# A graph network's set-up: edge words moved by xor and minimum, weights by predicated copies, x's norms in between

## The reference, cut to what matters

```
x: (6250, 256)   src, dst: (106250,) int32, sorted by dst   edge_weight: (106250,)
h   = layernorm(x)                       # rows: mean, variance, eps 1e-5
msg = logmap(h[src], h[dst]) * edge_weight[:, None]
agg = segment_sum(msg, dst)
u   = expmap(agg, h) ...                 # then a Mobius product with weight, bias
# three more layers: attention with a softmax per node, scores, a mean
```

## Time and profile before

| | us |
|---|---|
| three runs, median (lowest, highest) | 4950.73 (4947.53, 4952.23) |
| span of the profiled execution | 5717.0 |
| busy in it: PE, DVE, ACT, POOL | 3330.2, 3248.6, 1811.1, 3290.0 |
| mean granted TensorE clock | 0.754 of full |
| first gather, first sum added to A | 155.88, 240.59 |

### The profile page before, as it was taken

How to read it: one execution, slowest core, us unless ns; L and a number is a source line. 1 busy time by engine, 2 the same in 40 slices (tenths; PEclk the granted TensorE clock), 3 DMA queues, 4 the chain that set the end, 5 groups by cost and what they waited for, 6 DMA issues and landing times. The chain is left out here.

```text
span 5717.0 us, 56211 instructions
## 1 busy us (share of the span) xinstructions
PE 3330.2 (58%) x11120; PEld 2187.6 (38%) x11120; DVE 3248.6 (57%) x10255; ACT 1811.1 (32%) x4253; POOL 3290.0 (58%) x3410
## 2 busy tenths in 40 slices
PE   0477777777543555556554555555555556666555
PEld 0355555555431333333333333333333334333333
DVE  8677777777983555555566344444447344334435
ACT  2254444444692323333336322222226100000000
POOL 5566666666004666666653666666662466666664
PEclk8789988898875777776777767777777776667767
DMA  2444444443114333333333444444443433333333
GB/s 90 118 110 111 110 110 107 110 111 106 49 46 123 92 91 93 94 89 93 92 101 119 111 111 113 114 112 112 114 111 114 143 98 99 93 98 101 99 91 107
DMA packets 290665, 586.90 MB, mean 103 GB/s; under 512 B 63201, under 2 KB 170717, under 8 KB 290334
## 3 DMA queue, kind: packets, MB, share of 16 engines
q0 software_dynamic: 159456, 440.74, 29.6%
q1 hardware_dynamic: 100322, 108.64, 6.1%
q10 hardware_dynamic: 30556, 33.94, 2.1%
HBM read 530.98 MB, written 52.10 MB: 102 GB/s over the span
## 5 line engine op out<-in xcount | busy, mean ns | idle before, releaser
L519 POOL DMA_INDIRECT X<-table,src_tab x2490 | 2367.7, 951 | 1786.5 <-issue 690.4
L639 PE MATMUL psum<-X,onehot 128*128 128x259 f32 x4980 | 1906.8, 522 | 1245.7 <-DVE A L1280 570.9
L639 PEld LDWEIGHTS psum<-X,onehot 128*128 128x128 f32 x4980 | 1118.2, 251 | 1827.8 <-issue 1117.1
L1280 DVE SCALAR_TENSOR_TENSOR A<-A,psum 128x259 f32 x1660 | 701.7, 423 | 1315.4 <-remote 690.8
L1280 DVE SCALAR_TENSOR_TENSOR A<-A,same_tab,psum 128x259 f32 x1620 | 777.0, 480 | 613.4 <-remote 308.3
L509 POOL DMA_INDIRECT X<-table,src_tab x832 | 793.7, 954 | 534.0 <-issue 233.1
L780 ACT ACTIVATE onehot<-G,zero_col,ecols 128x128 f32<-128x128 bf16 x1660 | 697.3, 482 | 987.6 <-remote 325.5
L648 PE MATMUL psum<-H,G 128*128 x1664 | 602.9, 450 | 352.9 <-DVE G L1368 208.9
L626 PE MATMUL psum<-X,onehot 128*128 128x259 f32 x1664 | 559.3, 422 | 4.4 <-DVE A L1280 3.1
L648 PEld LDWEIGHTS psum<-H,G 128*128 128x128 f32 x1664 | 318.1, 215 | 545.5 <-issue 510.0
L780 ACT ACTIVATE onehot<-onehot,zero_col,coef 128x128 f32<-128x128 bf16 x832 | 350.6, 482 | 277.3 <-DVE coef L1411 83.7
(11 more groups left out here) (367 smaller groups left out, 2843.4 us busy)
## 6 DMA issues: line engine op xcount, KB each, us to landing
X<-table,src_tab POOLq DMA_INDIRECT x3322
plain<-rows_dram ACTq DMA_DIRECT2D x168, 160.0 KB
plain<-rows_dram SPq DMA_DIRECT2D x104, 256.0 KB
table<-H SPq DMA_DIRECT2D x21, 906.5 KB, 5.9
x_dram<-X SPq DMA_DIRECT2D x21, 896.0 KB, 4.1
X<-x_dram SPq DMA_DIRECT2D x14, 896.0 KB, 6.1
table<-A SPq DMA_DIRECT2D x7, 906.5 KB, 7.0
G<-x_dram SPq DMA_DIRECT2D x7, 896.0 KB
```

The costliest lines, as they stand in the source:

```text
L519: pool.indirect_dma_start(ring[:, s % SLOTS, :], None, table, bass.IndirectOffsetOnAxis(src_tab[:, s:s + 1], 0)).then_inc(sem(f"batch_in{s ...
L639: pe.matmul(psum[:, k % ACC_BANKS, 0:W], hots[:, k % HOTS, :], ring[:, k, :], start=True, stop=True).then_inc(sem("used"), 1)
L1280: stt(total, total, same, psum[:, t % ACC_BANKS, 0:W], ALU.mult, ALU.add).then_inc(sem("sum_added"), 1)
```

## The change

The words become positive f32 bit patterns: a mark at bit 29, an "empty" bit at 27 and the distance's seven bits in reverse order from bit 20 to 26, above the 13 bits of src. A level is an xor with its bit into `movers[i]` and a minimum of that with what stands at the place 2^i to the left. The level's mover is kept; ScalarE turns the seven into masks with a Relu (of -1 times the word plus a constant), and VectorE moves the weights by seven predicated copies, in place of GpSimd. The new fields() reverses the bits with integer operations on VectorE. Statistics, roots, norms and squares of x stand between the levels, in order 0 to 6; ScalarE squares five parts, VectorE two. dst goes out first on SP's queue, src on ScalarE's between x's parts 0 and 1; parts 2 to 6 wait for dst. The raw weights load early into onehot, are transposed before the words, and are copied by ScalarE, as are rows_out. GpSimd zeroes 3787 of A's 12691 columns. cuts_made and links_made, weight_columns and node_scalars run within g = -3, -2 and -1 of layer 0's loop, on VectorE; SP stores the cuts ahead of the fifth load of rows; VectorE waits for them before g = 0. The loop's own steps are as before.

```diff
+X2_ACT = 5 * UN
...
+MARK = 1 << 29
+EMPTY = 1 << 27
+TOP = 26
+ARRIVED = struct.unpack("f", struct.pack("I", MARK | 1 << TOP - 6))[0]
...
+            rows_in(sp, dst, dst_rows_i[:, :, 0:P], "dst_padded", 1, "dst_in")
...
+            sp.dma_start(wide["bb"], bias0.rearrange("(p d) -> p d", p=1).to_broadcast([P, D])).then_inc(sem("bias_in"), 16)
+            for n, w in enumerate((w0, w1, w_neigh, w_self)):
+                sp.dma_start(wraw[:, n], w.rearrange("(c p) d -> p c d", p=P)).then_inc(sem("raw_in"), 16)
+            rows_in(sp, edge_weight, w_rows[:, :, P:2 * P], "sums_zero", 1, "w_in")
...
+            for c in range(OUTER):
...
+                if f == 4:
+                    steps_out()
...
-            pool.memset(A[:, :, :], 0.0).then_inc(sem("sums_zero"), 1)
...
-                for i, low in enumerate(LOW):
-                    shift = 1 << i
-                    pool.wait_ge(sem("movers"), i + 1)
-                    pool.wait_ge(sem("w_kept"), 2 * i + 1)
-                    now, to = w_rows[:, :, low:], w_rows[:, :, low - shift:2 * P - shift]
-                    pool.tensor_copy(moved_w[i], movers[i]).then_inc(sem("w_taken"), 1)
-                    pool.wait_ge(sem("w_taken"), 2 * i + 1)
-                    pool.tensor_tensor(moved_w[i], now, moved_w[i], ALU.mult).then_inc(sem("w_taken"), 1)
-                    pool.wait_ge(sem("w_taken"), 2 * i + 2)
-                    pool.tensor_tensor(now, now, moved_w[i], ALU.subtract).then_inc(sem("w_kept"), 1)
-                    pool.wait_ge(sem("w_kept"), 2 * i + 2)
-                    pool.tensor_tensor(to, to, moved_w[i], ALU.add).then_inc(sem("w_kept"), 1)
...
+            pool.memset(a_flat[:, EW:2 * EW], 0.0).then_inc(sem("sums_zero"), 1)
+            pool.memset(a_flat[:, left:NB * W], 0.0).then_inc(sem("sums_zero"), 1)
...
+            x_part(0)
+            rows_in(act, src, src_rows_i, "src_padded", 1, "src_in")
+            x_part(1)
...
+            act.wait_ge(sem("dst_in"), 16 * (3 + EC))
+            for c in range(2, OUTER):
+                x_part(c)
...
+            for c in range(OUTER):
+                act.wait_ge(sem("rstd_ready"), c + 1)
                 for b in part(c):
                     norm_first(b)
+                if c + 1 < OUTER:
+                    root_first(c + 1)
...
+                if c == 2:
+                    act.wait_ge(sem("weights_turned"), 1)
+                    for n, name in enumerate(("w0T", "w1T", "wnT", "wsT")):
+                        ins = act.copy(wT[name][:, :, 0:D], psum[:, 4 + n, :].rearrange("p (c d) -> p c d", c=2))
+                    ins.then_inc(sem("weights_kept"), 1)
+
+            act.wait_ge(sem("words_moved"), 1)
+            for i in range(len(LOW)):
+                func(movers_f[i], movers_f[i], ACT.Relu, bias=col("t3")[:, i:i + 1], scale=-1.0).then_inc(sem("masks"), 1)
+            act.wait_ge(sem("dst_turned"), 1)
+            act.copy(rows_out[:, 0:4, :], psum[:, 0, :].rearrange("p (c e) -> p c e", c=4))
+            act.copy(rows_out[:, 4:6, :], psum[:, 1, 0:2 * P].rearrange("p (c e) -> p c e", c=2))
+            act.copy(rows_out[0:S - 6 * P, 6, :], psum[0:S - 6 * P, 1, 2 * P:3 * P]).then_inc(sem("rows_kept"), 1)
...
-            for i, low in enumerate(LOW):
-                shift = 1 << i
-                now, to = words[:, :, low:], words[:, :, low - shift:2 * P - shift]
-                taken = moved[:, 0:EC * (2 * P - low)].rearrange("p (c e) -> p c e", c=EC)
-                chain(ts(movers[i], now, SRC_BITS + i, 1, ALU.logical_shift_right, ALU.bitwise_and))
-                chain(tt(taken, now, movers[i], ALU.mult))
-                dve.sem_inc(sem("movers"), 1)
-                if i + 1 < len(LOW):
-                    chain(tt(now, now, taken, ALU.subtract))
-                    chain(tt(to, to, taken, ALU.add))
...
+            def fields():
+
+                SHL, SHR, AND, OR = ALU.logical_shift_left, ALU.logical_shift_right, ALU.bitwise_and, ALU.bitwise_or
+                dve.wait_ge(sem("dst_in"), 16 * (3 + EC))
+                chain(ts(delta_i, dst_rows_i[:, :, 0:P], P - 1, MARK >> SRC_BITS, AND, OR))
+                dve.tensor_copy(last_dst, dst_rows_i[:, :, P - 1])
+                tt(gone_i, dst_rows_i[:, :, 0:P], dst_rows_i[:, :, 1:P + 1], ALU.not_equal)
+                chain(ts(half_a, delta_i, 4, 0x70, SHL, AND))
+                chain(stt(half_a, delta_i, 4, half_a, SHR, OR))
+                chain(stt(half_a, delta_i, 8, half_a, AND, OR))
+                ts(half_b, half_a, 2, 0x44, SHL, AND)
+                chain(stt(delta_i, gone_i, EMPTY.bit_length() - 1 - SRC_BITS, delta_i, SHL, OR))
+                chain(stt(half_b, half_a, 0x2A, half_b, AND, OR))
+                chain(ts(half_a, half_a, 2, 0x11, SHR, AND))
+                chain(tt(half_b, half_b, half_a, OR))
+                chain(stt(delta_i, half_b, TOP - 6 - SRC_BITS, delta_i, SHL, OR))
+                dve.wait_ge(sem("src_in"), 16 * 3)
+                chain(stt(words[:, :, P:2 * P], delta_i, SRC_BITS, src_rows_i, SHL, OR))
+
+            def move(i):
+
+                low, shift = LOW[i], 1 << i
+                chain(ts(movers[i], words[:, :, low:], 1 << TOP - i, None, ALU.bitwise_xor))
+                to = words_f[:, :, low - shift:2 * P - shift]
+                chain(tt(to, to, movers_f[i], ALU.min))
...
             first_stats(0)
-            for n in range(1, OUTER):
-                first_stats(n)
-                first_rstd(n - 1)
-            first_rstd(OUTER - 1)
-
-            def add_left(out_, at, shift):
-
-                for a, z in tabs:
-                    b = a + shift
-                    ins = tt(out_[:, a:z], out_[:, a:z], psum[:, at + b // 512, b % 512:b % 512 + z - a], ALU.add)
-                return ins
+            first_rstd(0)
+            fields()
+            first_stats(1)
+            move(0)
+            first_rstd(1)
+            move(1)
+            first_stats(2)
+            move(2)
+            first_rstd(2)
+            move(3)
+            first_stats(3)
+            move(4)
+            first_rstd(3)
+            move(5)
+            first_stats(4)
+            move(6)
+            dve.sem_inc(sem("words_moved"), 1)
+            first_rstd(4)
+            first_stats(5)
+            first_rstd(5)
+            first_stats(6)
+            first_rstd(6)
...
+                from_next = psum[:, 2 + (a + 1) // 512, (a + 1) % 512:(a + 1) % 512 + z - a]
+                ts(arrived[:, a:z], from_next, ARRIVED, None, ALU.is_lt)
+                ins = tt(words_tab_f[:, a:z], words_tab_f[:, a:z], from_next, ALU.min)
...
+            chain(ts(field_tab, words_tab, SRC_BITS, MARK >> SRC_BITS, ALU.logical_shift_right, ALU.bitwise_xor))
+            chain(ts(dst_tab[:, :], field_tab, float(P), None, ALU.min))
+            dve.sem_inc(sem("tables_kept"), 1)
...
+            dve.wait_ge(sem("w_in"), 16 * 3)
+            for i, low in enumerate(LOW):
+                shift = 1 << i
+                dve.wait_ge(sem("masks"), i + 1)
+                if i:
+                    dve.wait_ge(sem("w_moved"), i)
+                dve.copy_predicated(w_rows[:, :, low - shift:2 * P - shift], movers[i], w_rows[:, :, low:]).then_inc(sem("w_moved"), 1)
+
+            dve.wait_ge(sem("x2_dve"), NB - X2_ACT)
+            dve.wait_ge(sem("x2_act"), X2_ACT)
+            dve.tensor_copy(col("x2"), H[:, :, AUX2])
+            dve.sem_inc(sem("rows0_free"), 1)
...
+            for a, z in tabs:
+                ins = dve.copy_predicated(w_tab[:, a:z], arrived[:, a:z],
+                                          psum[:, 4 + (a + 1) // 512, (a + 1) % 512:(a + 1) % 512 + z - a])
+            chain(ins)
+            dve.wait_ge(sem("table_stored"), 16 * OUTER)
+            dve.tensor_copy(H[:, :, AUX], col("x2")).then_inc(sem("own_squares"), 1)
...
+            def cuts_made():
+                dve.wait_ge(sem("rows_kept"), 1)
+                chain(dve.memset(cuts_out, 0.0))
+                tt(cuts_out[:, 0:EC - 1, 1:P], rows_out[:, 0:EC - 1, 1:P], rows_out[:, 0:EC - 1, 0:P - 1], ALU.not_equal)
+                n = S - (EC - 1) * P
+                chain(tt(cuts_out[0:n, EC - 1, 1:P], rows_out[0:n, EC - 1, 1:P], rows_out[0:n, EC - 1, 0:P - 1], ALU.not_equal))
+                ts(cuts_out, cuts_out, -BIG, None, ALU.mult)
...
+            bias_scaled()
             for g in range(-3, NG0):
+                if g == 0:
+                    dve.wait_ge(sem("steps_out"), 16 * (EC + 1))
                 if g >= 0:
...
+                    if g == -3 and k == 12:
+                        cuts_made()
+                        links_made()
+                    if g == -2 and k == 12:
+                        weight_columns()
+                    if g == -1 and k == 0:
+                        node_scalars()
```

More of the change, by code:

```diff
@@ L9 @@
+import struct
 from contextlib import ExitStack
@@ L237, in gnn_program @@
-        o += EC * P // 2
```

(45 more changed lines are left out.)

270 lines of the change are left out of this document (114 added, 156 removed).

## The result

The changed kernel takes 4917.36 us (four runs, 4916.38 to 4919.76) against 4950.69 (four runs): a ratio of 0.9935, 95% interval 0.9922 to 0.9947. It is 33 us faster, where 71 were forecast, and lies outside the range of 4852 to 4902. This time the profiled execution's span, 4914.3 us, is as long as the runs.

The account below looks back on a forecast made before the run. Layer 0's loop start was taken as the bound: set-up terms summed to a first addition at 150.3 against 219.5 without stalls, 69.2 us, taken as 71. So 4950.7 - 71 = 4880 us, range 4852 to 4902.

Parts of the forecast that it names:

- The bound: Layer 0's loop: its start, the first addition at 240.59, decides; GpSimd's 24.89 us wait at the full ring confirms it.
- Rival 3: Layer 0's gathers pace it, so only their stream's 59.6 us earlier start is won: 4891 us, chance 0.12.
- A term put at nothing: Layer 0's loop and all behind it: taken as untouched, so no change of time was counted there.
- The words: VectorE's set-up: 66.4 + 4.4 us removed, 17.6 for levels and 12.1 for fields() added, 41 us less.
- When fields() starts: VectorE's set-up: fields() at 24.5 us, about as now (24.09), with bounds 20 and 29; ScalarE free at 22.4.
- Squares, masks, copies: Set-up before layer 0: ScalarE's seventh square ends at 80.7; masks cost nothing; seven predicated copies 8.6 us, upper bound 17.
- The stalls: Before layer 0's loop: without stalls of 6.4 and 14.7 us the start is 219.5; change worth 69.2, or 90.3 if real.

Follow-up runs that it names:

- the second profile: The kernel before, unchanged, run and profiled again beside the kernel after on one chip: 4953.35 us, with a span of 4951.5.
- tt_on_pool: The kernel after with one cast and one multiplication of 32 columns added on GpSimd behind its memsets: 4895.11 us, 0.9889 of the kernel before.
- no_pool_moves: The kernel before without GpSimd's weight moves, so layer 0's weights are other numbers: 4940.8 us, 0.9978 of the kernel before.
- x_by_sp: The kernel after with x's parts 2 to 6 and the tail issued by SP behind dst instead of by ScalarE: 4903.46 us, 0.99.

## Why the prediction was wrong

Two steps failed, and both stand in one sentence: "Layer 0's loop, and all behind it, is untouched, so the change is worth what it moves the loop's start".

**The bound: wrong.** I took the 24.89 us wait at the full ring for the sign that the loop's start decides, and it belonged to a profiled execution 766 us longer than the runs. Undisturbed, that wait is 2.38 us, gathers follow each other with 0.30 between them through the whole layer, and the stream's start decides. Rival 3 described it, with 59.6 us and a chance of 0.12; measured are 55.5 and the 2 of the ring's wait. I had asked of each stall whether a run without profiler has it, and removed the stalls from the set-up, but not from the loop's pace, where they hid the bound. The first profile's view of the gathers has them:

```profile
L509 POOL DMA_INDIRECT X<-table,src_tab x832: 940/946/1838, 155.9 to 1431.5; - x167
...
  PE psum L626: 157.5, 72
  remote: 92.3, 43
```

That is 1.54 us from gather to gather, where it is 1.26 in the second profile.

**A term put at nothing: the step that cost most.** The loop's instructions are the same, but not their durations. I costed the removal of GpSimd's weight moves as a gain in contention only; it also changed what GpSimd had run before the gathers, and that made each gather dearer. Of the start's gain, 12.7 us are lost within layer 0 (10.6 in the table, and the ring's wait that is gone) and 11.9 within layers 1 to 3. The sum is then 55.5 + 2.1 - 12.7 + 1.0 - 11.9 = 34.0, of 33.9.

**What each was worth.** From the 71 to the 34, 1.8 is what I had put on top of 69.2 for the stalls; 5.8 is the loop's start, 63.4 earlier and not 69.2; 5.8 is the bound, 57.6 for the stream and the ring in place of 63.4; 23.6 is the dearer gathers, less the 1.0 won between layers 0 and 1. With the bound wrong and the gathers at their old price the time would have been 4950.7 - 57.6 = 4893, within the range. tt_on_pool is that kernel: its gathers have the old medians, and it is 57.9 us faster than the kernel before on its chip (4953.0 - 4895.1).

**The words: right.** Levels at 1.08 to 1.55 an operation, fields() 11.9 from 31.63 to 43.53 (12.1 in the sum), and no_pool_moves shows the contention by itself: 30.6 of the 66.4 us.

**When fields() starts: mis-sized.** 31.6, not 24.5, and past the bound of 29. ScalarE was free at 29.6, not at 22.4: dst, for which it waits behind the first part of x, was in at 13.67, not at 10.5, and five parts and the tail then took 15.9 us, not 11.9. Of the 7.2 us, 3.2 are dst's and 4.0 the issues'. Through ScalarE's other work 7 us became 5: last rstd at 86.1 (forecast 81.1), src_tab done at 90.4 (85.1), first gather 101.4 (96.3). x_by_sp shows what waiting for these issues costs in all, 14 us.

**Squares, masks, copies: right.** ScalarE ends the chain of x (3.60 us idle before the last rstd, as laid out). The masks take 7.32 from 90.0, beside VectorE's work, and VectorE has only 0.22 idle before the copies; what the masks would have cost on VectorE, no run tried. The seven copies take 9.87 against 8.6, at 17 the range's end was far. The first addition is at 155.7 to 156.5 against 150.3: 5 of it from fields().

**The stalls: right.** 219.5 was the estimate of the undisturbed start, 219.89 is what the new profile shows. They were the profile's, neither kernel has them.

## What to carry to other kernels

A profile that is much longer than the runs is to be taken again before any bound is read from it: its stalls fall on all engines, but they hide best the one that works at a fixed pace. Look then for an engine whose gaps are all equal; where there is one, count from its first instruction and not from where its results are used. And work that is taken off an engine may change what its other instructions cost, as it did here, where that was two thirds of the miss: compare the medians of unchanged instructions first.

## What the runs showed of the hardware that was not expected

A gather issued by GpSimd takes 957 ns in the median (951 at the least) when only iotas, a select and memsets ran before it, and 946 (942) once a cast or a two-input operation has run, also with a memset behind the cast. The 49 scalings that GpSimd does between layers 1 and 2 raise 946 to 953 and leave 957 as it is; a cast and a product behind them bring it back to 946. By the medians tt_on_pool should win 1662 gathers at 11 ns and 1660 at 4, an estimate of 25 us, and it won 22 to 26. Why is open: the runs show what sets the duration, not what it is inside GpSimd, and the cast alone or the product alone behind the scalings was not tried.

ScalarE issued the first two parts of x (at 0.81 and 4.14 us) in 0.43 and 0.41 us. Of the five parts from 13.67 on, the first two took 0.40 and 0.50 and the next three 3.16, 4.90 and 4.33, then the tail 2.15; what such an issue waits for the profile does not show. In x_by_sp the same six issues take SP 1.2 to 3.2 us each. What stands behind them on the engine's list, here one square root on ScalarE's, waits for all of them.
